# The relation bias in threshold form: each hinge as a scaled relu(d - t) or max(d, t)

## The chip, the core and the metric

The kernel runs on one NeuronCore of a Trainium2 chip. A core has five engines, each with its own queue of instructions, which wait for one another by semaphores: TensorE (PE, matrix products into PSUM), VectorE (DVE), ScalarE (ACT), GpSimd (POOL) and SyncE (SP, which here only issues DMAs). The metric is the device time of one execution in microseconds.

## The reference

A block in two stages over 16 batches of 128 rows with 128 features. The first stage runs four layers of cross attention (16 heads of 64) with a feed-forward part; the second one a self attention with a mixture of experts. The change touches one term of the first stage, the bias that is added to the scores of every head:

```python
def _attention(x, src, dist, bias, Wq, Wk, Wv, Wo, Wth, bth, Wto, bto):
    ...
    hbias = jax.nn.relu(dist[..., None] @ Wth + bth)      # 32 hinges a layer
    qs_bias = (hbias @ Wto + bto)[..., 0]
    logits = jnp.einsum('btnh,bfnh->bnft', k, q)
    logits = logits + bias + qs_bias[:, None]
    w = jax.nn.softmax(logits, axis=-1)
```

For each pair of rows with distance d the bias is the sum over k of 32 hinges w_k relu(a_k d + b_k), plus one constant and the mask. The values a, b, w differ by layer; `dist` and `mask` are the same in all four layers.

## The kernel before

All data is fp32. The first stage walks 64 units (layer by batch) in 16 groups of 4 batches. A step (g, i) works on unit i of group g, together with the projections of the unit after it and the output and feed-forward parts of the two units before it; each engine has its own list of what it does in a step, written out by hand. `walk` unrolls group 0 and the last group, and loops over the 14 between, so each engine takes a branch back at the end of a group. I call i = 0 the first step of a group, i = 1 and 2 the middle ones, i = 3 the last one.

While group g is in work, the bias of group g + 1 (4 batches, so tiles of 128 partitions by 512) is made in small parts placed among the other work:

- 24 hinges (`VEC_K`) go by way of ScalarE and VectorE. `relu` (L780) makes `relu_z = Relu(scale * dist_g + bias)` with scale and bias each a column of `cst`, into 6 slots. `term` (L938) on VectorE adds `weight * relu_z` to `bias_acc`: the first as a tensor_scalar with two column operands (L948), the other 23 as scalar_tensor_tensor, called fused below (L951). `Z_PLAN` and `TERM_PLAN` say how many of them stand at each of five places of a step; a group's first two terms stand at the second place of its first step.
- 8 hinges (`POOL_K`) go to GpSimd, two in each step: `product` (L1404, times a w, plus b w), `clamp` (L1412, min and max with bounds that are 0 or huge by the sign of w), `add` (L1419, into `pool_acc`, which begins from the mask).
- `finish_bias` (L982), the last that VectorE does in a last step, adds `bias_acc` and `pool_acc` into `bias`.

For group 0, which has no attention beside it, ScalarE and VectorE take 26 hinges and GpSimd 6.

GpSimd's other work stands in the same queue: four `norm` per step (L1393), which scale the exponentials of a quad of heads by VectorE's `inverse` (rinv, L1006), and the roots of the layer norms. VectorE's `score_quad` (L990) adds the bias to a quad's scores and finds the maximum; ScalarE's `exps` (L796) waits for it, and `inverse` waits for `exps`.

SyncE copies a layer's columns into `cst` per group: distances and a, b first (`load_dist`), GpSimd's columns next, then, when the bias of the group before is done, w and the mask (`load_wto`). At the start it loads the constants, the distances and x, waits for the constants, copies their columns, loads mask and context, and goes on to the weights.

Of the kernel before, what the change touches and what calls it, by code (L numbers as in the profile page):

```python
# [18 lines left out]
ALU = mybir.AluOpType  # L19
ACT = mybir.ActivationFunctionType  # L20
AX_X = mybir.AxisListType.X
# [23 lines left out]
START_VEC_K = 26  # L45
START_POOL_SKIP = START_VEC_K - VEC_K
POOL_FIRST = 2
Z_SLOTS = 6
# [18 lines left out]
Z_BEFORE = START_VEC_K - 1 - START_Z[-1][-1]  # L67
TERMS_BEFORE = START_VEC_K - 1 - START_TERMS[-1][-1]
# [3 lines left out]
def vec_count(g, k):  # L72

    return k if isinstance(g, int) and g == 0 else g * VEC_K + (START_VEC_K - VEC_K + k)

def pool_count(g, k):

    return k - START_POOL_SKIP if isinstance(g, int) and g == 0 else g * POOL_K + (k - START_POOL_SKIP)

def z_slot(g, k):
    return (k if isinstance(g, int) and g == 0 else START_VEC_K + k) % Z_SLOTS

C_WTH, C_BTH, C_WTO = 0, BIAS_K, 2 * BIAS_K
C_BTO = 3 * BIAS_K
C_PW, C_PB, C_HI, C_LO = [C_BTO + 1 + n * BIAS_K for n in range(4)]
C_ALL = C_BTO + 1 + 4 * BIAS_K  # L90
# [32 lines left out]
def block_program(nc, x, ctx_in, dist, mask, g_xattn, g_ffn, Wq, Wk, Wv, Wo, Wth, bth, Wto, bto,  # L123
                  Wf1, bf1, Wf2, bf2, W_qkv, b_qkv, W_gate, b_gate, W_experts, b_experts, out):
    with ExitStack() as stack:
# [32 lines left out]
        clamp_in = sb("clamp_in", [P, 2, GROUP * P])  # L158
        clamped = sb("clamped", [P, 2, GROUP * P])
        pool_acc = sb("pool_acc", [P, GROUP, P])  # L160
# [79 lines left out]
        cst_in, cst_mul, cst_ready, dist_in, cv_in, cp_in = [sem(n) for n in ("cst_in", "cst_mul", "cst_ready", "dist_in", "cv_in", "cp_in")]  # L240
        z_done, term_done, bias_done = sem("z_done"), sem("term_done"), sem("bias_done")
        pool_mul, pool_clamp, pool_sum = sem("pool_mul"), sem("pool_clamp"), sem("pool_sum")
# [60 lines left out]

        def layer_of(g, i):

            return (g + i // GROUP) >> 2
# [3 lines left out]
        def _(sp):  # L310
# [12 lines left out]
            def load_dist(g):  # L323

                load_dist_rows(g)
                load_cst(g, C_WTH, C_WTO, dist_in)

            def load_wto(g):

                load_cst(g, C_WTO, C_PW, cv_in)  # L330
                load_mask(g)
# [45 lines left out]
            for w, col in ((Wth.rearrange("l o k -> o l k"), C_WTH), (bth.rearrange("(o l) k -> o l k", o=1), C_BTH),  # L377
                           (Wto.rearrange("l k o -> o l k"), C_WTO)):
# [36 lines left out]
            wait_first(sp, consts, z_done, START_VEC_K)  # L415
# [1127 lines left out]
```

## Time and profile before

| what | value |
|---|---|
| time, median of 3 runs | 1392.51 us (1392.48 to 1393.23) |
| span of the profiled execution, first to last instruction | 1391.1 us |
| median less span, what lies around it | 1.4 us |
| TensorE busy | 1246.5 us, 90% |
| VectorE busy | 1221.8 us, 88% |
| ScalarE busy | 1062.8 us, 76% |
| GpSimd busy | 833.3 us, 60% |
| granted TensorE clock, mean | 0.968 |

A busy share is an average over stages with different limits, and a matmul's end is modelled, so a high share alone names no bound. The chain that ended last is shared out as 23% TensorE, 23% "issue", 23% VectorE, 18% ScalarE and 2% GpSimd: no engine holds it alone. The table and the chain are for the whole run; what one group and one step look like is in the rows below.

### The profile page before, as it was taken

Reading aid. Unit: us, or ns where it says so; the run is one execution under the profiler, and the core shown is the slowest. Engines: PE = TensorE matmul, PEld = TensorE weight load, DVE = VectorE, ACT = ScalarE, POOL = GpSimd, SP = SyncE. Lnnn points to the kernel's source line nnn. Section 1 sums busy time; section 2 is a strip of 40 time slices with the busy share of each in tenths; the row PEclk is TensorE's granted clock in tenths of the full one; section 3 lists DMA queues with packets and bytes.
Section 4 is the critical chain, followed back from the end, with each engine's and each line's share of the span. In section 5 each row is a group of like instructions: output and inputs, shape, how many; then the busy total and the mean of one; then the engine's idle time right before and its main releaser. Section 6 shows DMA issues by size and latency. Waiting matters only on the chain.

```text
span 1391.1 us, 39815 instructions
## 1 busy us (share of the span) xinstructions
PE 1246.5 (90%) x11184; PEld 1035.3 (74%) x11184; DVE 1221.8 (88%) x4922; ACT 1062.8 (76%) x3353; POOL 833.3 (60%) x889
## 2 busy tenths in 40 slices
PE   1599989898989899998989898989898999799998
PEld 1377878787878787787778787878777877677776
DVE  4899989898989899998989898989898988579886
ACT  4588868787878788787878787868687866478886
POOL 3677767676767677776767676767676753111110
PEclk9799999999999999999999999999999999999999
DMA  5201000102110100021100000111101000000000
GB/s 152 67 7 31 15 27 12 29 12 76 44 31 12 31 12 22 20 67 39 35 16 16 25 13 29 57 48 27 31 12 42 12 12 9 5 23 19 23 14 9
DMA packets 69115, 41.04 MB, mean 30 GB/s; under 512 B 14840, under 2 KB 63872, under 8 KB 68992
## 3 DMA queue, kind: packets, MB, share of 16 engines
q1 hardware_dynamic: 68992, 39.84, 9.9%
q14 instruction: 99, 0.81, 0.2%
q8 instruction: 24, 0.39, 0.1%
HBM read 23.29 MB, written 1.05 MB: 17 GB/s over the span
## 4 chain that ended last, share of the span: by engine, by line
PE 23%; issue 23%; DVE 23%; ACT 18%; POOL 2%; DVEq 1%; DMA 1%; ACTq 0%; SPq 0%; POOLq 0%
ACT prob L802 10%; DVE bias_acc L951 4%; PE L L688 4%; ACT relu_z L785 4%; PE O L552 3%; PE M L582 3%; DVE score L998 3%; DVE qT L1123 3%; DVE hid L1073 3%; PE M L762 2%; DVE st L1016 2%; PE M L628 2%; PE T L695 2%; PE M L560 2%; ACT probT L809 1%
## 5 line engine op out<-in xcount | busy, mean ns | idle before, releaser
L802 ACT ACTIVATE prob<-score,nmax 128x128 f32<-128x128 f32 x1024 | 396.6, 390 | 182.4 <-DVE nmax L998 182.2
L1396 POOL TENSOR_TENSOR prob<-prob,rinv 128x512 f32<-128x512 f32 x256 | 293.5, 1146 | 232.1 <-DVE rinv L1006 229.7
L951 DVE SCALAR_TENSOR_TENSOR bias_acc<-relu_z,cst,bias_acc 128x512 f32<-128x512 f32 x370 | 339.1, 917 | 9.7 <-ACT relu_z L785 0.2
L785 ACT ACTIVATE relu_z<-dist_g,cst 128x512 f32<-128x512 f32 x386 | 295.0, 804 | 17.2 <-DMA cst<-cst_all 16.9
L998 DVE CUSTOM_DVE_ANT_0 score<-L,bias 128x128 f32<-128x128 f32 x1024 | 233.6, 281 | 4.0 <-PE L L528 1.5
L802 ACT ACTIVATION_READ_ACCUMULATOR prob<-score,nmax 128x1 f32 x1024 | 193.3, 189 | 0.0
L1391 POOL TENSOR_TENSOR sd<-mv,half 128x1 f32<-128x1 f32 x128 | 105.5, 824 | 120.3 <-DVE mv L1018 117.6
L538 PE MATMUL T<-ident,prob 128*128 128x128 f32 x1024 | 164.4, 285 | 4.9 <-POOL prob L1396 4.0
L552 PEld LDWEIGHTS O<-probT,v 128*64 128x64 f32 x2048 | 109.3, 136 | 60.0 <-issue 52.4
L582 PE MATMUL M<-wv,ctxT 128*128 128x512 f32 x256 | 144.1, 645 | 7.8 <-DVE hid L1073 5.1
L528 PE MATMUL L<-kT,qT 64*128 64x128 f32 x2048 | 148.7, 285 | 0.0
L667 PEld LDWEIGHTS M<-wo,oT 128*128 128x128 f32 x1024 | 124.1, 192 | 30.6 <-issue 29.8
L560 PE MATMUL M<-hT,wq 128*128 128x128 f32 x1024 | 127.8, 279 | 20.5 <-DVE v L1106 20.5
L1428 POOL TENSOR_TENSOR pool_acc<-pool_acc,clamped 128x512 f32<-128x512 f32 x110 | 141.5, 1286 | 5.4
L560 PE MATMUL M<-ctxT,wk 128*128 128x128 f32 x1024 | 141.2, 283 | 3.8 <-issue 2.6
L552 PE MATMUL O<-probT,v 128*64 128x128 f32 x2048 | 140.1, 279 | 4.2 <-issue 2.9
L528 PEld LDWEIGHTS L<-kT,qT 64*128 64x128 f32 x2048 | 124.3, 187 | 21.2 <-issue 20.9
L560 PEld LDWEIGHTS M<-hT,wq 128*128 128x128 f32 x1024 | 120.9, 194 | 24.9 <-issue 24.9
L538 PEld LDWEIGHTS T<-ident,prob 128*128 128x128 f32 x1024 | 121.4, 146 | 22.0 <-POOL prob L1396 11.1
L628 PE MATMUL M<-h2T,wf 128*128 128x128 f32 x512 | 84.4, 315 | 58.8 <-DVE h2T L1059 58.8
L560 PEld LDWEIGHTS M<-ctxT,wk 128*128 128x128 f32 x1024 | 131.2, 200 | 4.8 <-issue 2.9
L1409 POOL TENSOR_SCALAR clamp_in<-dist_g,cst 128x512 f32<-128x512 f32 x126 | 120.1, 953 | 21.2 <-DMA cst<-cst_all 21.2
(134 smaller groups left out, 2282.8 us busy)
## 6 DMA issues: line engine op xcount, KB each, us to landing
dist_g<-in_fside_BxSxS SPq DMA_DIRECT2D x16, 256.0 KB, 2.8
mask_g<-in_mask_Bx1x1xS_ff SPq DMA_DIRECT2D x16, 256.0 KB, 3.3
ctxT<-ctxT_all SPq DMA_DIRECT2D x64, 64.0 KB, 1.9
xs<-x_all SPq DMA_DIRECT2D x64, 64.0 KB, 1.8
x_all<-xs SPq DMA_DIRECT2D x64, 64.0 KB, 1.8
wk<-in_L_xattn_Wk SPq DMA_DIRECT2D x4, 512.0 KB, 3.6
wv<-in_L_xattn_Wv SPq DMA_DIRECT2D x4, 512.0 KB, 4.7
wq<-in_L_xattn_Wq SPq DMA_DIRECT2D x4, 512.0 KB, 5.1
```

What stands on the lines that cost most here:

```text
L528: last = mm(L[r][:, m * P:(m + 1) * P], qT[64 * r:64 * r + 64, s, j, :], kT[64 * r:64 * r + 64, s, j, :], start=True, stop=True)
L538: last = nc.tensor.transpose(T[c % 2][:, m * P:(m + 1) * P], prob[:, c, m, :], ident[:, :])
L552: last = mm(O[64 * r:64 * r + 64, m * P:(m + 1) * P], v[:, i % 2, n * HD:(n + 1) * HD], probT[:, 2 * octet + r, m * P:(m + 1) * P], start= ...
L560: last = mm(dst[:, m * P:(m + 1) * P], w[:, j * P:(j + 1) * P], src, start=True, stop=True)
L582: mm((M0 if a else M1)[:, :], ctxT[:, i % 2, :], wv[:, a * 512:(a + 1) * 512], start=True, stop=True).then_inc(v_done, 1)
L667: last = mm(M2[:, 0:P], oT[:, (i - 1) % 2, j, :], wo[:, j, :], start=j == 0, stop=j == PAIRS - 1)
L785: nc.scalar.activation(relu_z[:, z_slot(g, k), :], dist_g[:, :, :], ACT.Relu, bias=cst[:, C_BTH + k:C_BTH + k + 1], scale=cst[:, C_WTH + k ...
L802: last = nc.scalar.activation(prob[:, c, m, :], score[:, c, m, :], ACT.Exp, bias=nmax[:, c, m:m + 1], scale=-1.0, accum_out=rsum[:, c, m:m ...
L951: vec.scalar_tensor_tensor(out=bias_acc[:, :], in0=relu_z[:, z_slot(g, k), :], scalar=weight, in1=bias_acc[:, :], op0=ALU.mult, op1=ALU.ad ...
L998: last = vec.tensor_tensor_reduce(out=score[:, c, m, :], in0=L[c % 2][:, m * P:(m + 1) * P], in1=bias[:, i % GROUP, :], scale=-1.0, scalar ...
L1396: gp.tensor_tensor(prob[:, c, :, :], prob[:, c, :, :], rinv[:, c, :].rearrange("p (m o) -> p m o", o=1).broadcast_to([P, 4, P]), ALU.mult) ...
L1428: gp.tensor_tensor(pool_acc[:, :, :], so_far[:, :, :], clamped[:, k % 2, :].rearrange("p (b t) -> p b t", b=GROUP), ALU.add).then_inc(pool ...
```

## The change

With t = -b / a a hinge with a > 0 is w a relu(d - t), and one with a < 0 is w |a| (relu(d - t) - (d - t)). So every hinge becomes c relu(d - t) with c = |a| w, and the parts linear in d of the falling ones are gathered in one slope `AL` and one constant `BE` per layer. On GpSimd relu(d - t) is written as max(d, t) - t, with the -t also gathered in `BE`. Hinges with a nearly 0 go whole into the constant.

- VectorE makes the new columns once, for all four layers, before the first term: 22 small instructions on up to 128 x 128, with 13 waits among them, in place of 4.
- ScalarE's relu has the constant 1.0 as its scale, and a column as its bias as before.
- VectorE's sum starts with `begin`: `AL * dist_g + mask_g` as a fused instruction; then 24 fused terms. The last sum becomes a fused one that adds `BE`.
- GpSimd makes each hinge by one tensor_scalar (max with t, times c); the first goes straight into `pool_acc`, the 7 others are added. `product` is gone, and `clamp`s stand earlier in a step.
- Group 0 is split 24 to 8 as the others are, and reads its columns straight from `cst_all`, so that SyncE copies none for it and doesn't wait for the constants.

```diff
-            wait_first(sp, consts, cst_in, 64)
-            load_cst(0, C_WTH, C_WTO, dist_in)
-            load_wto(0)
+            load_mask(0)
             sp.dma_start(c_raw[:, :, :], ctx_in.rearrange("b t d -> t b d")).then_inc(c_in, 16)
-            wait_first(sp, consts, cst_ready, 4)
-            load_cst(0, C_PW, C_ALL, cp_in)
             load_k(0)
...
-                wait(act, term_done, vec_count(g, k + 1 - Z_SLOTS))
-                nc.scalar.activation(relu_z[:, z_slot(g, k), :], dist_g[:, :, :], ACT.Relu, bias=cst[:, C_BTH + k:C_BTH + k + 1],
-                                     scale=cst[:, C_WTH + k:C_WTH + k + 1]).then_inc(z_done, 1)
+                    if isinstance(g, int) and g == 0:
+                        act.wait_ge(cst_ready, 1)
+                wait(act, term_done, term_count(g, k + 1 - Z_SLOTS) if k >= Z_SLOTS else term_count(g, k - Z_SLOTS))
+                nc.scalar.activation(relu_z[:, k % Z_SLOTS, :], dist_g[:, :, :], ACT.Relu,
+                                     bias=hinges(g)[:, C_NT + k:C_NT + k + 1], scale=1.0).then_inc(z_done, 1)
...
+            dve.wait_ge(cst_step, 6)
+            vec.reciprocal(inverse_, whole).then_inc(cst_step, 1)
+            dve.wait_ge(cst_step, 8)
+            vec.tensor_tensor(cols(C_NT), edge, inverse_, ALU.mult).then_inc(cst_ready, 1)
...
+            def begin(g):
+                dve.wait_ge(cv_in, g * 32 + 16)
+                dve.wait_ge(dist_in, g * 32 + 16)
+                if isinstance(g, int) and g == 0:
+                    dve.wait_ge(cst_ready, 4)
+                wait(dve, bias_done, g)
+                vec.scalar_tensor_tensor(out=bias_acc[:, :], in0=dist_g[:, :, :].rearrange("p b t -> p (b t)"),
+                                         scalar=hinges(g)[:, C_AL:C_AL + 1],
+                                         in1=mask_g[:, :, :].rearrange("p b t -> p (b t)"), op0=ALU.mult,
+                                         op1=ALU.add).then_inc(term_done, 1)
...
-                if k == 0:
-                    vec.tensor_scalar(bias_acc[:, :], relu_z[:, z_slot(g, k), :], weight, cst[:, C_BTO:C_BTO + 1], ALU.mult,
-                                      ALU.add).then_inc(term_done, 1)
+                vec.scalar_tensor_tensor(out=bias_acc[:, :], in0=relu_z[:, k % Z_SLOTS, :], scalar=hinges(g)[:, C_C + k:C_C + k + 1],
+                                         in1=bias_acc[:, :], op0=ALU.mult, op1=ALU.add).then_inc(term_done, 1)
...
                     for k in TERM_PLAN[i][q] if i < GROUP else ():
+                        if k == 0:
+                            begin(g + 1)
                         term(g + 1, k)
...
-                vec.tensor_tensor(bias[:, :, :], bias_acc[:, :].rearrange("p (b t) -> p b t", b=GROUP),
-                                  pool_acc[:, :, :], ALU.add).then_inc(bias_done, 1)
+                vec.scalar_tensor_tensor(out=bias[:, :, :].rearrange("p b t -> p (b t)"), in0=bias_acc[:, :],
+                                         scalar=hinges(g)[:, C_BE:C_BE + 1], in1=pool_acc[:, :], op0=ALU.add,
+                                         op1=ALU.add).then_inc(bias_done, 1)
...
             def clamp(g, k):
+                if k == 0:
+                    wait_first(pool, consts, dist_in, g * 32 + 16, bias_done, g, cp_in, g * 16)
+                    if isinstance(g, int) and g == 0:
+                        pool.wait_ge(cst_ready, 2)
+                        pool.wait_ge(cst_step, 10)
+                else:
+                    wait_first(pool, consts, pool_sum, sum_count(g, max(k - 2, 0)))
+                held = hinges(g)
+                gp.tensor_scalar(clamped[:, k % 2, :] if k else pool_acc[:, :], dist_g[:, :, :].rearrange("p b t -> p (b t)"),
+                                 held[:, C_PT + k:C_PT + k + 1], held[:, C_PT + POOL_K + k:C_PT + POOL_K + k + 1],
+                                 ALU.max, ALU.mult).then_inc(pool_clamp, 1)
...
                 if bias_too:
-                    product(g + 1, 2 * i)
                     clamp(g + 1, 2 * i)
                 if cur:
                     norm(g, i, 0)
                 if bias_too:
                     add(g + 1, 2 * i)
-                    product(g + 1, 2 * i + 1)
+                    clamp(g + 1, 2 * i + 1)
                 if cur:
                     norm(g, i, 1)
                 if bias_too:
-                    clamp(g + 1, 2 * i + 1)
                     add(g + 1, 2 * i + 1)
```

SyncE's wait before the distances of the next group gains `term_done` (that `begin` has read them), beside the relus and the clamps.

## Rows read from the trace of the kernel before

**Rows 1.** Stretch table, a middle step: us, busy us by engine (instructions), clock, DMA

```profile
664.43:680.93 16.50, 16.13 (x150) 13.59 (x150) 15.91 (x66) 14.26 (x46) 12.45 (x14) 1.00 0.04 12
```

**Rows 2.** Timeline of VectorE and TensorE, one first step: start, us, engine, line

```profile
844.65 0.18 DVE L1006 RECIPROCAL rinv<-rsum 128x4 f32<-128x4 f32 x1 [2.36 <-issue]
...
862.73 1.16 PE L628 MATMUL M<-h2T,wf 128*128 128x128 f32 x8 [0.20 <-DVE h2T L1059]
```

**Rows 3.** Timeline, the same first step: ScalarE and VectorE around quad 2

```profile
851.25 0.60 ACT L839 ACTIVATE v<-M 128x512 f32<-128x512 f32 x1 [1.16 <-PE O L552]
...
854.24 1.52 ACT L785 ACTIVATE relu_z<-dist_g,cst 128x512 f32<-128x512 f32 x2
...
854.81 0.29 DVE L998 CUSTOM_DVE_ANT_0 score<-L,bias 128x128 f32<-128x128 f32 x1
...
857.33 0.18 DVE L1006 RECIPROCAL rinv<-rsum 128x4 f32<-128x4 f32 x1 [0.39 <-ACT prob L802]
```

**Rows 4.** Timeline of ScalarE in the second stage: with and without pointer scale

```profile
1291.55 1.59 ACT L906 ACTIVATE qm<-M,bq_mask,head_mask 128x128 f32<-128x128 f32 x4
...
1292.91 1.26 ACT L872 ACTIVATE prob<-L,nmaxF 128x128 f32<-128x128 f32 x4
```

**Rows 5.** Timeline, the first step again: VectorE's first two terms, GpSimd beside them

```profile
850.66 1.32 DVE L948 TENSOR_SCALAR bias_acc<-relu_z,cst 128x512 f32<-128x512 f32 x1
...
852.11 1.05 DVE L951 SCALAR_TENSOR_TENSOR bias_acc<-relu_z,cst,bias_acc 128x512 f32<-128x512 f32 x1
...
850.40 1.29 POOL L1428 TENSOR_TENSOR pool_acc<-mask_g,clamped 128x512 f32<-128x512 f32 x1
...
851.68 0.94 POOL L1409 TENSOR_SCALAR clamp_in<-dist_g,cst 128x512 f32<-128x512 f32 x1
```

**Rows 6.** Timeline, a middle step: VectorE and GpSimd around norm 2

```profile
675.61 0.18 DVE L1006 RECIPROCAL rinv<-rsum 128x4 f32<-128x4 f32 x1
...
676.82 0.79 DVE L951 SCALAR_TENSOR_TENSOR bias_acc<-relu_z,cst,bias_acc 128x512 f32<-128x512 f32 x1
...
678.76 0.74 DVE L951 SCALAR_TENSOR_TENSOR bias_acc<-relu_z,cst,bias_acc 128x512 f32<-128x512 f32 x1
...
673.94 0.76 POOL L1416 TENSOR_SCALAR clamped<-clamp_in,cst 128x512 f32<-128x512 f32 x1
...
674.78 1.28 POOL L1428 TENSOR_TENSOR pool_acc<-pool_acc,clamped 128x512 f32<-128x512 f32 x1
...
676.02 1.04 POOL L1396 TENSOR_TENSOR prob<-prob,rinv 128x512 f32<-128x512 f32 x1
```

**Rows 7.** Timeline of VectorE from the start to the first bias

```profile
11.49 0.29 DVE L934 TENSOR_TENSOR cst_all<-cst_all 128x128 f32<-128x128 f32 x1 [11.49 <-DMA cst_all<-in_L_xattn_bto]
...
17.58 0.55 DVE L948 TENSOR_SCALAR bias_acc<-relu_z,cst 128x512 f32<-128x512 f32 x1 [5.33 <-ACT relu_z L785]
...
18.30 2.33 DVE L951 SCALAR_TENSOR_TENSOR bias_acc<-relu_z,cst,bias_acc 128x512 f32<-128x512 f32 x3 [0.17 <-ACT relu_z L785]
...
28.49 0.25 DVE L1042 RECIPROCAL ln_rs<-ln_sd 128x16 f32<-128x16 f32 x1 [0.45 <-POOL ln_sd L1518]
...
30.28 3.20 DVE L951 SCALAR_TENSOR_TENSOR bias_acc<-relu_z,cst,bias_acc 128x512 f32<-128x512 f32 x3
...
33.39 0.29 DVE L1016 BATCH_NORM_STATS2 st<-xs 128x6 f32<-128x128 f32 x1
...
57.50 0.69 DVE L987 TENSOR_TENSOR bias<-bias_acc,pool_acc 128x512 f32<-128x512 f32 x1
```

**Rows 8.** The page: DMA issues (us to landing); costliest groups (busy us, mean ns)

```profile
L951 DVE SCALAR_TENSOR_TENSOR bias_acc<-relu_z,cst,bias_acc 128x512 f32<-128x512 f32 x370 | 339.1, 917 | 9.7 <-ACT relu_z L785 0.2
...
xs<-x_all SPq DMA_DIRECT2D x64, 64.0 KB, 1.8
```

More of the change, by code:

```diff
@@ L66, with z_count, term_count, clamp_count @@
 F_FIRST_PARTS = [[0, 1], [2, 3, 4], [5, 6], [7, 8, 9], [10, 11]]
-Z_BEFORE = START_VEC_K - 1 - START_Z[-1][-1]
-TERMS_BEFORE = START_VEC_K - 1 - START_TERMS[-1][-1]
+Z_BEFORE = VEC_K - 1 - START_Z[-1][-1]
+TERMS_BEFORE = VEC_K - 1 - START_TERMS[-1][-1]
 STATS_TERMS = (4, 8)
[L72 to L87, printed above, removed]
-C_BTO = 3 * BIAS_K
-C_PW, C_PB, C_HI, C_LO = [C_BTO + 1 + n * BIAS_K for n in range(4)]
-C_ALL = C_BTO + 1 + 4 * BIAS_K
+def z_count(g, k):
+    return g * VEC_K + k
+def term_count(g, k):
+    return g * (VEC_K + 1) + 1 + k
+def clamp_count(g, k):
+    return g * POOL_K + k
+def sum_count(g, k):
+    return g * (POOL_K - 1) + k
+C_A, C_B, C_W = 0, BIAS_K, 2 * BIAS_K
+C_BTO = 3 * BIAS_K
+C_NT = C_BTO + 1
+C_C = C_NT + BIAS_K
+C_AL = C_C + BIAS_K
+C_BE = C_AL + 1
+C_PT = C_BE + 1
+C_ALL = C_PT + 2 * POOL_K
 E_HEADS = 16
@@ L302, in f_there, with hinges @@
             return not isinstance(g, int) or 0 <= GROUP * g + i < BATCHES
+        def hinges(g):
+            return cst_all[:, 0, :] if isinstance(g, int) and g == 0 else cst
         def layer_of(g, i):
@@ L931, in cols, with magnitude @@
                 return cst_all[:, :, a:a + BIAS_K]
+            slope, edge, weight = cols(C_A), cols(C_B), cols(C_W)
+            size, live, kept, whole, inverse_, falling, share, flat = [t[:, :, :] for t in prep]
+            def magnitude(out, of):
+                return vec.scalar_tensor_tensor(out=out, in0=of, scalar=-1.0, in1=of, op0=ALU.mult, op1=ALU.max)
             dve.wait_ge(cst_in, 64)
-            vec.tensor_tensor(cols(C_PW), cols(C_WTH), cols(C_WTO), ALU.mult).then_inc(cst_ready, 1)
@@ new lines, in _ @@
+            magnitude(flat, slope).then_inc(cst_step, 1)
+            dve.wait_ge(cst_step, 2)
+            vec.tensor_scalar(size, size, FLAT, TINY, ALU.mult, ALU.max).then_inc(cst_step, 1)
+            dve.wait_ge(cst_step, 3)
+            vec.tensor_tensor(live, size, flat, ALU.is_lt).then_inc(cst_step, 1)
+            dve.wait_ge(cst_step, 4)
+            vec.tensor_tensor(kept, slope, live, ALU.mult).then_inc(cst_step, 1)
+            dve.wait_ge(cst_step, 5)
+            vec.scalar_tensor_tensor(out=whole, in0=live, scalar=0.0, in1=kept, op0=ALU.is_equal, op1=ALU.add).then_inc(cst_step, 1)
@@ L1398, in norm @@
                                  ALU.mult).then_inc(normed, 1)
-            def first_k(g):
-                return START_POOL_SKIP if isinstance(g, int) and g == 0 else 0
-            def product(g, k):
-                col = VEC_K + k
-                wait_first(pool, consts, *((dist_in, (g + 1) * 32, cp_in, (g + 1) * 16) if k == first_k(g) else ()),
-                           pool_clamp, pool_count(g, k - 1))
-                gp.tensor_scalar(clamp_in[:, k % 2, :], dist_g[:, :, :], cst[:, C_PW + col:C_PW + col + 1],
-                                 cst[:, C_PB + col:C_PB + col + 1], ALU.mult, ALU.add).then_inc(pool_mul, 1)
@@ L1435, in step @@
                 if i == -1:
-                    for k in range(START_POOL_SKIP + POOL_FIRST, POOL_K):
-                        product(0, k)
+                    for k in range(POOL_FIRST, POOL_K):
                         clamp(0, k)
```

106 lines of the change are left out of this document (59 added, 47 removed).

## The prediction

> **What bounds the kernel now.** The page's busy shares come first: they call both TensorE and VectorE nearly full, so only a single step can say which wait ends last. The stretch table of a middle step of a group comes second [rows 1]: of 16.50 us TensorE works 16.13, VectorE 15.91, ScalarE 14.26 and GpSimd 12.45. VectorE's missing 0.6 us are short pauses between an instruction and the one that reads its result, so VectorE sets these steps and TensorE stands 0.37 us behind it. The timelines come third. At the start of a group's first step [rows 2] VectorE sits idle 2.36 us for "issue", at the back edge of its loop; no edit of the change is meant for that. TensorE runs on until it meets a gap of only 0.20 us, waiting for VectorE's h2T. So in the first step TensorE is 0.20 us from being the bound, and what makes VectorE late there is ScalarE [rows 3]: VectorE idles 0.39 us at 857.33 for the exponentials of quad 2, and ScalarE, released by TensorE at 851.25, worked without a pause up to them, with two relus (854.24, 1.52 us) just ahead.
>
> So I ask of every edit: does it shorten VectorE's own row of work in a middle or last step, or ScalarE's in a first step? All else is covered.
>
> **ScalarE: the relu loses its per-partition scale.** No row shows a relu with a pointer bias and a constant scale. The nearest pair [rows 4] is 128x128: four instructions with pointer bias and pointer scale take 1.59 us, four with pointer bias and constant scale 1.26, so 0.33 in three start-to-start distances and one tail: 0.08 to 0.11 each. I take 0.09; the bounds are 0 (512 elements could hide it) and 0.11. Over 24 relus and 15 prepared groups that is 32 us of ScalarE, but only the two relus before quad 2's exponentials stand on the path of a first step: 0.18 us. The scores that these exponentials also need are done at about 855.1 (854.81 + 0.29), so they could start 0.18 us sooner. VectorE then goes on that much sooner and TensorE's 0.20 us gap nearly closes; past it TensorE bounds the step. With 14 groups: -2.5 us (0 to -2.8). In middle steps the exponentials wait for VectorE's scores, and a faster ScalarE is worth nothing.
>
> **VectorE: one fused instruction more per group.** The tensor_scalar of term 0 becomes two fused ones, `begin` and term 0. A fused one alone takes 0.74 [rows 6], beside GpSimd up to 1.32 [rows 5]. That is 0.7 us more on the engine that sets most steps, 15 times, if nothing covers it. But the neighbours change. Now GpSimd's add (850.40, 1.29) and product (851.68, 0.94) run beside the pair, and the tensor_scalar ends only after the add does [rows 5]; the pair takes 2.50 us, to 853.16. After, a group's first add is gone and one clamp of about 0.77 stands there: `begin` should end at about 851.75, and two fused ones alone, 0.78 apart [rows 7], bring VectorE to about 853.4. Bounds for the three: 2.3 us (all alone) and 4.2 (each 1.32, with the pause of 0.13 that stands before 852.11). I take 2.75, near the lower end, since only one GpSimd instruction is left beside them. Up to about 0.5 us later nothing is lost, for VectorE idles 0.39 us at 857.33 and 0.1 us in two small waits before it. So: 0. If that cover is gone, each 0.1 us costs 14 x 0.1 = 1.4.
>
> **GpSimd: 15 instructions a group instead of 24.** Eight products and one add leave. Its time is worth nothing at 75% of a step; what counts is when norms start and what VectorE meets. Between norms 0 and 1 an add and a two-pointer tensor_scalar remain, as now. Between norms 1 and 2 the clamp (673.94, 0.76) goes and the add (674.78, 1.28) moves up. Norm 2 now starts only when that add ends (676.02); then it can start once VectorE's rinv (675.61, 0.18) is there, about 0.15 us sooner, and the term at 676.82 no longer meets its tail: 0.74 instead of 0.79 [rows 6]. That is 0.05 us on the engine that sets the step, in 2 steps of 14 groups: -1.4 us (0 to -1.4). In last steps VectorE is later and I count 0. What leaves before norm 0 stands beside VectorE work that reads PSUM, and counts 0 too.
>
> **The final sum** becomes a fused one: 0.69 us [rows 7] against 0.74. It is VectorE's last before the back edge, 16 times 0.05: 0.8 us, or 0 if the 2.36 us of "issue" run meanwhile; I take +0.2.
>
> **The start.** SyncE loses three copies of constants and its waits for them, so the mask, the context and the first weights are issued earlier, behind x in the same queue; VectorE's own work decides when the first step can begin. It starts when the constants have landed, at 11.49 [rows 7]. Instead of 4 small instructions it runs 22, most reading the one before: at the 0.29 of that row 6.4 us. A reciprocal of 128 elements is in no row; it lies between 0.29 and 8 times the 0.25 of one of 16, and at 1.0 makes 7.1 together. Relu 0 waits behind the ninth of them instead of a copy, which is no later. `begin` starts at 18.6, where term 0 started at 17.58. Five fused ones 0.78 apart end at 22.5, where the first four terms ended at 20.6: 1.9 us late. That carries to the normalised x: 32.2 instead of 30.28. But then one term follows where three did (3.20 us), and the first moments wait for a load of x that takes 1.8 us [rows 8]: 34.1 against 33.39. From there the same work runs to the first bias at 57.50. So +0.7 us. 
>
> **New waits.** GpSimd's clamp 0 waits for the previous bias, with norm 0 queued behind it; norm 0 needs scores of that bias, so it waits longer anyway. SyncE's next load of distances waits for `begin`, long past by then. `begin` waits for the mask where term 0 did. All 0.
>
> **Sum.** -2.5 - 1.4 + 0 + 0.2 + 0.7 = -3.0 on the span of 1391.1: 1388.1. The median of the runs is 1.4 above that span: 1389.5 us.
>
> **Rivals.** *Nothing measurable.* TensorE is 0.20 to 0.37 us behind VectorE everywhere, and the start is my softest term: with 2.5 us more there, or with the 0.18 or the 0.05 absent, the sum is between 0 and -2: 1390.5 to 1392.5. Against it: the wait of 0.39 us for ScalarE.
>
> *Less contention frees VectorE.* The 370 fused ones average 917 ns [rows 8] against 740 alone: 65 us lost beside GpSimd. If that fell with GpSimd's bias instructions, 9 of 24, it would be 24 us: 1368, or some 1380 where TensorE's 0.20 to 0.37 us a step caps it. Against it: by the timelines what goes does not stand beside fused ones in middle and last steps. It is also what the Trainium skill would have one expect (GPSIMD Engine Reference, Key points): GpSimd shares its SBUF interfaces with VectorE and contends with instructions that have two SBUF inputs. The stretched rows agree; whether it pays depends on which neighbours go.
>
> *ScalarE was the bound.* Then 32 us would go: 1360. Its 2.2 us without work in a middle step speak against it.
>
> *Slower: VectorE's extra instruction isn't covered.* If `begin` and term 0 both come out at 1.32, the three take 3.5 instead of 2.50; 0.5 of that is past the cover, 14 x 0.5 = +7, the relus' gain is lost behind it, and with -1.4 + 0.2 + 0.7 it is 1399. For it speak the 917 ns; against it the one short clamp beside three instructions. It decides from 3.2 us on for the three.
>
> **Chances.** Forecast 0.45 (its own range 1387.5 to 1391), nothing measurable 0.32, contention 0.08, ScalarE 0.02, slower 0.13. A change of 0.2%, 2.8 us, is about what can be told from none: the line is 1389.7. Of the forecast some 0.32 lies below it and 0.13 above. Faster 0.32 + 0.08 + 0.02 = 0.42; same 0.13 + 0.32 = 0.45; slower 0.13. The range leaves out most of the contention case, ScalarE's and the far half of the slower one: 1385 to 1396.
>
> **What would show it.** In the profile after: relus about 0.09 us shorter; in first steps the wait before quad 2's rinv down from 0.39 to about 0.2 and TensorE's gap before its reader of h2T near 0; middle steps 16.45 instead of 16.50; `begin` near 1.05 us; first moments near 34 us. I am wrong if `begin` and the two terms take over 3.2 us, if middle steps lengthen, if the pause at the back edge changes, or if the first bias comes more than 3 us later than now.

## The result and the profile after

| | before | after |
|---|---|---|
| time, median of 4 runs each | 1392.49 us (1386.82 to 1393.23) | 1410.78 us (1407.41 to 1414.15) |
| ratio after / before | | 1.0152, 95% interval 1.0121 to 1.0183 |
| profiled execution, span | 1391.1 us | 1408.2 us |
| busy TensorE, VectorE | 1246.5, 1221.8 us | 1256.1, 1233.5 us |
| busy ScalarE, GpSimd | 1062.8, 833.3 us | 1029.6, 875.9 us |

The change is slower by 18 us, outside the range of 1385 to 1396. Three groups of the changed kernel, by form (busy us, mean ns of one, idle time before and what ended it):

```profile
L1008 DVE SCALAR_TENSOR_TENSOR bias_acc<-relu_z,cst,bias_acc 128x512 f32<-128x512 f32 x360 | 317.0, 881 | 13.4
L799 ACT ACTIVATE relu_z<-dist_g,cst 128x512 f32<-128x512 f32 x360 | 243.0, 712 | 5.1 <-DMA cst<-cst_all 5.1
L1471 POOL TENSOR_SCALAR clamped<-dist_g,cst 128x512 f32<-128x512 f32 x105 | 237.2, 2259 | 0.0
```

Two things stand out. The relu fell by 0.09 us, as forecast, from 804 to 712 ns. But GpSimd's new clamp, which I priced at 0.77 us, takes 2.26. The fused terms even got shorter (917 in [rows 8], now 881), so longer terms don't explain the loss.

Where the time is can be read from the steps. I measure them from one copy of hT on VectorE to the next: four a group. The first two, taken together below, hold a group's end, the back edge and the first step; the other two are the middle steps. The stretch table of two groups (us, busy us by engine, granted clock of TensorE):

```profile
546.10:586.29 40.19, 35.30 (x301) 29.58 (x300) 34.08 (x133) 26.89 (x91) 26.28 (x21) 0.92 0.09 25
619.69:658.67 38.98, 34.11 (x301) 28.86 (x300) 33.94 (x133) 26.88 (x91) 26.29 (x21) 0.96 0.14 41
586.29:603.08 16.79, 16.13 (x151) 13.60 (x150) 16.09 (x67) 13.77 (x47) 13.28 (x11) 1.00 0.04 12
603.08:619.69 16.61, 16.28 (x151) 13.62 (x150) 16.00 (x66) 14.38 (x48) 13.38 (x11) 1.00 0.32 107
```

A middle step was 16.50 us [rows 1]. Now it is 16.79 and 16.61, and TensorE's work in the first has not grown: 16.13 us, as before. The pairs are 38.98 in one group and 40.19 in the other, 38.9 before on average, and they differ in the clock: the granted 0.92 and 0.96 stand for (1 - 0.92) x 2 x 40.19 = 6.4 and 3.1 us at 1.2 instead of 2.4 GHz. The clock record of the profile, which is finer, has 6.8 us in five of 13 groups and 3.4 in the others; before it was one of 13.

VectorE's timeline in a middle step shows what got longer:

```profile
667.70 0.18 DVE L1079 BATCH_NORM_AGGREGATE mv<-st 128x2 f32<-128x6 f32 x1
667.89 0.75 DVE L1008 SCALAR_TENSOR_TENSOR bias_acc<-relu_z,cst,bias_acc 128x512 f32<-128x512 f32 x1
...
670.95 0.18 DVE L1067 RECIPROCAL rinv<-rsum 128x4 f32<-128x4 f32 x1
671.14 0.75 DVE L1008 SCALAR_TENSOR_TENSOR bias_acc<-relu_z,cst,bias_acc 128x512 f32<-128x512 f32 x1
...
672.39 0.48 DVE L1092 TENSOR_SCALAR h<-xs,mv,rs 128x128 f32<-128x128 f32 x1
672.98 0.29 DVE L1059 CUSTOM_DVE_ANT_0 score<-L,bias 128x128 f32<-128x128 f32 x1
```

No instruction here is longer than before, but they start later: the two terms 0.19 us after the start of the short instruction ahead of them (0.12 before), and a score 0.11 us after the end of h, where it used to start 0.08 us ahead of that end. The kernel before, at the same h and score:

```profile
664.80 0.49 DVE L1031 TENSOR_SCALAR h<-xs,mv,rs 128x128 f32<-128x128 f32 x1
665.21 0.28 DVE L998 CUSTOM_DVE_ANT_0 score<-L,bias 128x128 f32<-128x128 f32 x1
```

No line of another engine ends these pauses. What fills the first two is not in these views, which leave out register operations and waits. The trace has them (and nothing new ahead of the score, whose pause stays open):

```
start us  us     VectorE's queue, from mv to the term behind it
kernel before
660.198   0.182  mv
660.233   0.040  register operation, carries the wait on the term before
660.318   0.787  term
changed kernel
667.696   0.182  mv
667.722   0.040  register operation
667.809   0.040  register operation, carries the wait on the term before
667.894   0.752  term
```

Here each register operation puts the next instruction 0.085 us further back. Over the whole run VectorE has 1210 of them, 874 before: 336 more, which is 24 terms x 14 looped groups.

They come from the counts in the waits. Before, terms and relus were both counted 24 a group, so the number that one term waits for on the relus is the number that the next waits for on the terms, and one register served both. `begin` now signals `term_done` as well: terms run at 25 a group, relus at 24, and in the loop, where the group is a register, each term needs a second value.

The first step and the start of the changed kernel:

```profile
855.07 0.18 DVE L1067 RECIPROCAL rinv<-rsum 128x4 f32<-128x4 f32 x1 [2.33 <-issue]
...
860.84 0.90 DVE L1000 SCALAR_TENSOR_TENSOR bias_acc<-dist_g,cst,mask_g 128x512 f32<-128x512 f32 x1
861.87 1.63 DVE L1008 SCALAR_TENSOR_TENSOR bias_acc<-relu_z,cst,bias_acc 128x512 f32<-128x512 f32 x2
...
867.74 0.18 DVE L1067 RECIPROCAL rinv<-rsum 128x4 f32<-128x4 f32 x1 [0.21 <-ACT prob L816]
...
873.48 1.16 PE L640 MATMUL M<-h2T,wf 128*128 128x128 f32 x8 [0.35 <-DVE h2T L1120]
```

```profile
17.89 0.75 DVE L1000 SCALAR_TENSOR_TENSOR bias_acc<-dist_g,cst_all,mask_g 128x512 f32<-128x512 f32 x1
...
33.16 0.29 DVE L1077 BATCH_NORM_STATS2 st<-xs 128x6 f32<-128x128 f32 x1 [1.26 <-DMA xs<-x_all]
...
53.21 4.98 DVE L1008 SCALAR_TENSOR_TENSOR bias_acc<-relu_z,cst_all,bias_acc 128x512 f32<-128x512 f32 x4
58.29 0.75 DVE L1047 SCALAR_TENSOR_TENSOR bias<-bias_acc,cst_all,pool_acc 128x512 f32<-128x512 f32 x1
```

The kernel before, its last four terms ahead of the first bias:

```profile
54.29 3.11 DVE L951 SCALAR_TENSOR_TENSOR bias_acc<-relu_z,cst,bias_acc 128x512 f32<-128x512 f32 x4
```

`begin` and two terms take 2.66 us (forecast 2.75), the wait for quad 2's exponentials is 0.21 instead of 0.39 [rows 3], and the pause at the back edge is what it was [rows 2]. But TensorE's gap before its reader of h2T is 0.35, not near 0: VectorE lost what ScalarE had gained. The first bias comes 0.8 us later, though the first moments come 0.23 us sooner than before (33.16 against 33.39 [rows 7]).

### The profile page after: what moved, and what is told of

The parts are those of the page before. It is cut to its first block, busy times and chain, and to the rows that moved or that the text cites. A ratio compares the mean times of both kernels' runs of the same rounds, so it can differ in the third digit from the quotient of the medians.

```text
span 1408.2 us, 39902 instructions
## 1 busy us (share of the span) xinstructions
PE 1256.1 (89%) x11184; PEld 1044.1 (74%) x11184; DVE 1233.5 (88%) x4954; ACT 1029.6 (73%) x3351; POOL 875.9 (62%) x751
## 3 DMA queue, kind: packets, MB, share of 16 engines
q1 hardware_dynamic: 68560, 38.62, 9.6%
## 4 chain that ended last, share of the span: by engine, by line
DVE 29%; issue 25%; PE 25%; ACT 14%; POOL 3%; DVEq 2%; DMA 2%; ACTq 0%; SPq 0%; POOLq 0%
ACT prob L816 9%; DVE bias_acc L1008 5%; DVE score L1059 5%; PE L L700 4%; PE M L640 3%; PE M L572 3%; DVE qT L1184 3%; PE M L594 2%; DVE st L1077 2%; PE O L564 2%; PE M L774 2%; DVE hid L1134 2%; PE T L707 2%; DVE probT L1098 2%; ACT relu_z L799 2%
## 5 line engine op out<-in xcount | busy, mean ns | idle before, releaser
L1457 POOL TENSOR_TENSOR prob<-prob,rinv 128x512 f32<-128x512 f32 x256 | 279.1, 1090 | 220.2 <-DVE rinv L1067 220.2
L1008 DVE SCALAR_TENSOR_TENSOR bias_acc<-relu_z,cst,bias_acc 128x512 f32<-128x512 f32 x360 | 317.0, 881 | 13.4
L799 ACT ACTIVATE relu_z<-dist_g,cst 128x512 f32<-128x512 f32 x360 | 243.0, 712 | 5.1 <-DMA cst<-cst_all 5.1
L1471 POOL TENSOR_SCALAR clamped<-dist_g,cst 128x512 f32<-128x512 f32 x105 | 237.2, 2259 | 0.0
L1452 POOL TENSOR_TENSOR sd<-mv,half 128x1 f32<-128x1 f32 x128 | 111.5, 871 | 119.3 <-DVE mv L1079 113.7
L572 PE MATMUL M<-ctxT,wk 128*128 128x128 f32 x1024 | 146.7, 290 | 4.1 <-issue 2.7
L1481 POOL TENSOR_TENSOR pool_acc<-pool_acc,clamped 128x512 f32<-128x512 f32 x112 | 149.4, 1334 | 0.6
L572 PEld LDWEIGHTS M<-ctxT,wk 128*128 128x128 f32 x1024 | 136.3, 207 | 5.2 <-issue 3.0
```

The costliest lines, as they stand in the source:

```text
L572: last = mm(dst[:, m * P:(m + 1) * P], w[:, j * P:(j + 1) * P], src, start=True, stop=True)
L799: nc.scalar.activation(relu_z[:, k % Z_SLOTS, :], dist_g[:, :, :], ACT.Relu, bias=hinges(g)[:, C_NT + k:C_NT + k + 1], scale=1.0).then_inc ...
L1008: vec.scalar_tensor_tensor(out=bias_acc[:, :], in0=relu_z[:, k % Z_SLOTS, :], scalar=hinges(g)[:, C_C + k:C_C + k + 1], in1=bias_acc[:, :] ...
L1457: gp.tensor_tensor(prob[:, c, :, :], prob[:, c, :, :], rinv[:, c, :].rearrange("p (m o) -> p m o", o=1).broadcast_to([P, 4, P]), ALU.mult) ...
L1471: gp.tensor_scalar(clamped[:, k % 2, :] if k else pool_acc[:, :], dist_g[:, :, :].rearrange("p b t -> p (b t)"), held[:, C_PT + k:C_PT + k ...
L1481: gp.tensor_tensor(pool_acc[:, :], pool_acc[:, :], clamped[:, k % 2, :], ALU.add).then_inc(pool_sum, 1)
```

## The experiments

My theory at first was the slow clamp: it makes norm 1 start late, and VectorE meets it more often. The rivals: `begin` itself, the second register of each term, the start. Times below are ratios to the kernel before, run on the same chip, with 95% intervals.

**GpSimd's pairs of operations, by themselves**, e1. A small kernel of its own, no part of the reference:

```diff
+            for rep in range(2):
+                for (a, b), r in zip(PAIRS, res):
+                    gp.tensor_scalar(r[:, :], d[:, :], c[:, 0:1], c[:, 1:2] if b else None, op(a), *([op(b)] if b else [])).then_inc(made, 1)
+                    n += 1
+                    pool.wait_ge(made, n)
...
```

> This kernel computes nothing of the reference: with nothing beside it GpSimd runs a 128x512 tensor_scalar with thirteen pairs of operations, each twice and each waiting for the one before. If the pair (max, mult) is slow by itself, it takes about 2.07 us here as well, and (mult, add) and (min, max) about 0.76. If it is slow in the changed kernel only because VectorE runs beside it, all three take 0.76 here.

Five of its groups (mean ns behind the comma; r_max_None has one operation only):

```profile
L61 POOL TENSOR_SCALAR r_max_mult<-d,c 128x512 f32<-128x512 f32 x2 | 4.1, 2067 | 0.2
...
L61 POOL TENSOR_SCALAR r_max_None<-d,c 128x512 f32<-128x512 f32 x2 | 3.1, 1564 | 0.2
...
L61 POOL TENSOR_SCALAR r_mult_mult<-d,c 128x512 f32<-128x512 f32 x2 | 1.5, 770 | 0.2
L61 POOL TENSOR_SCALAR r_mult_add<-d,c 128x512 f32<-128x512 f32 x2 | 1.5, 768 | 3.9 <-DMA c<-in_L_xattn_Wth 3.8
...
L61 POOL TENSOR_SCALAR r_min_max<-d,c 128x512 f32<-128x512 f32 x2 | 1.5, 762 | 0.2
```

The pair is slow by itself. Four pairs take 0.76 to 0.77 us: (mult, add), (add, mult), (mult, mult), (min, max). Seven take 2.07 to 2.08: (max, mult), (mult, max), (max, add), (add, max), (max, min), (min, mult), (subtract, max). One operation alone takes 1.56. So two of the old instructions, 1.53, cost less than the new one. VectorE did (max, mult) twice in the same kernel, at 0.55 each.

**The changed kernel with a quick pair**, e2.

```diff
-                                 ALU.max, ALU.mult).then_inc(pool_clamp, 1)
+                                 ALU.mult, ALU.add).then_inc(pool_clamp, 1)
```

> The changed kernel with (mult, add) in the place of (max, mult) in GpSimd's clamp, so that its eight hinges of each layer come out as d times one column plus another; all else as it is. If the slow pair is the cause, the clamp falls from 2.26 us to 0.95 or less, norm 1 of a middle step starts within 0.25 us of its rinv again, and the time is 1387 to 1394 us. If VectorE's additional fused instruction or the new start is the cause, it stays at 1405 us or more.

1411.16 us, ratio 1.0148 (1.0119 to 1.0176). The clamp fell to 0.96 us, GpSimd's busy time by 149 us, and nothing happened: middle steps 16.79 and 16.61 again. My first theory is gone.

**The kernel before with the slow pair**, e3.

```diff
-                gp.tensor_scalar(clamped[:, k % 2, :], clamp_in[:, k % 2, :], cst[:, C_HI + col:C_HI + col + 1],
-                                 cst[:, C_LO + col:C_LO + col + 1], ALU.min, ALU.max).then_inc(pool_clamp, 1)
+                gp.tensor_scalar(clamped[:, k % 2, :], clamp_in[:, k % 2, :], cst[:, C_PB + col:C_PB + col + 1],
+                                 cst[:, C_PW + col:C_PW + col + 1], ALU.max, ALU.mult).then_inc(pool_clamp, 1)
```

> The kernel before with (max, mult) in the place of (min, max) in its clamp, on the columns of the product, so that its eight hinges of each layer are other numbers; all else as it is. If the slow pair costs by itself, its clamp goes from 0.82 us to 2.1 or more, and the time is 1402 us or more, since two clamps stand in each step as in the changed kernel. If the other edits of the change make the loss, it stays at 1391 to 1395.

1450.73 us, ratio 1.0433 (1.0403 to 1.0462), middle steps 17.77. So the slow pair can cost much more than the change lost, in an order in which 24 of GpSimd's bias instructions a group stand among the norms; in the changed kernel there are 15, and e2 shows that it costs nothing there. What is late here I did not follow.

**The kernel before with relus that have the constant scale**, e4, the first term of the sum alone.

```diff
-                                     scale=cst[:, C_WTH + k:C_WTH + k + 1]).then_inc(z_done, 1)
+                                     scale=1.0).then_inc(z_done, 1)
```

> The kernel before with 1.0 as the scale of its relus (bias still a column), so that its 24 hinges of ScalarE are relu(d + b); all else as it is. By the prediction's first term the relus get 0.09 us shorter, the wait before quad 2's rinv in first steps goes from 0.39 to about 0.2 us, and the time falls by 2.5 us, to about 1390. If TensorE bounds the first steps anyway, or something else is late next, it stays within 1 us of the kernel before.

1390.70 us, ratio 0.9994 (0.9978 to 1.0010): relus of 711 ns, but -2.5 us and nothing are both inside the interval, so the time doesn't decide. The profile shows the mechanism: the wait before quad 2's rinv falls to 0.21, and TensorE's gap before its reader of h2T from 0.19 to 0.01 (mean of 13 first steps).

```profile
855.97 0.18 DVE L1006 RECIPROCAL rinv<-rsum 128x4 f32<-128x4 f32 x1 [0.21 <-ACT prob L802]
```

**`begin` on a semaphore of its own**, e5: terms are counted 24 a group again. The waits of SyncE and ScalarE on these counts (not shown) are rewritten to match.

```diff
-    return g * (VEC_K + 1) + 1 + k
+    return g * VEC_K + k
...
-                                         op1=ALU.add).then_inc(term_done, 1)
+                                         op1=ALU.add).then_inc(begun, 1)
...
-                dve.wait_ge(term_done, term_count(g, k))
+                if k == 0:
+                    dve.wait_ge(begun, g + 1)
+                else:
+                    dve.wait_ge(term_done, term_count(g, k))
```

> The changed kernel, but begin signals a semaphore of its own, so that the counts of terms and of relus are both 24 a group, as in the kernel before; the same instructions on every engine otherwise. Theory: the 24th-against-25th count made VectorE's queue work out a second register for the waits of each term (336 register operations more in the trace). Then they are gone, middle steps are back at 16.5 us and the time is 1388 to 1396 us. If begin itself, 0.99 us on VectorE, is the cause, the time stays at 1405 or more.

1388.85 us, ratio 0.9978 (0.9963 to 0.9992): all of the loss is gone, and this version beats both kernels, the one before by 0.2%. VectorE's queue has 336 register operations fewer (308 single ones and 28 fused with others); the other engines have as many of these and of waits as in the changed kernel. Its stretches, pair and middle steps of one group:

```profile
610.59:649.14 38.55, 34.11 (x301) 28.81 (x300) 33.92 (x133) 26.90 (x91) 26.56 (x21) 0.96 0.14 41
649.14:665.63 16.49, 16.14 (x151) 13.60 (x150) 15.92 (x67) 13.77 (x47) 13.18 (x11) 1.00 0.17 44
665.63:682.10 16.47, 16.08 (x151) 13.59 (x150) 15.89 (x66) 14.38 (x48) 13.26 (x11) 1.00 0.04 12
```

Its timeline at the two terms, each 0.12 us behind the start of the short one, and h with the score 0.08 us ahead of its end:

```profile
658.17 0.18 DVE L1082 BATCH_NORM_AGGREGATE mv<-st 128x2 f32<-128x6 f32 x1
658.29 0.75 DVE L1011 SCALAR_TENSOR_TENSOR bias_acc<-relu_z,cst,bias_acc 128x512 f32<-128x512 f32 x1
...
661.36 0.18 DVE L1070 RECIPROCAL rinv<-rsum 128x4 f32<-128x4 f32 x1
661.48 0.77 DVE L1011 SCALAR_TENSOR_TENSOR bias_acc<-relu_z,cst,bias_acc 128x512 f32<-128x512 f32 x1
...
662.74 0.49 DVE L1095 TENSOR_SCALAR h<-xs,mv,rs 128x128 f32<-128x128 f32 x1
663.15 0.28 DVE L1062 CUSTOM_DVE_ANT_0 score<-L,bias 128x128 f32<-128x128 f32 x1
```

**The kernel before with two counts**, e6: the reverse, alone.

```diff
+def term_count(g, k):
+    more = 1 if k >= 1 else 0
+    return k + more if isinstance(g, int) and g == 0 else g * (VEC_K + 1) + (START_VEC_K - VEC_K + k + more)
...
-                    dve.wait_ge(term_done, vec_count(g, k))
+                    dve.wait_ge(term_done, term_count(g, k))
...
-                                      ALU.add).then_inc(term_done, 1)
+                                      ALU.add).then_inc(term_done, 2)
```

> The kernel before with the count of its terms raised by 2 at a group's first term, so that it runs at 25 a group beside 24 for the relus; nothing else is changed, and no engine's arithmetic. By the theory of the second register it loses what the change lost: 336 register operations more, middle steps of 16.6 to 16.8 us, 1402 to 1410 us. If begin or GpSimd's clamp is the cause, it stays at 1391 to 1395.

1406.33 us, ratio 1.0104 (1.0080 to 1.0128). An edit of a count alone costs 14 us: 308 register operations more on VectorE (22 terms of 14 groups here) and not one on another engine, middle steps of 16.61.

**e5 with the quick pair**, e7, whose edit is that of e2, and **e5 without `begin`**, e8, which also leaves out SyncE's wait for it.

```diff
-                        if k == 0:
-                            begin(g + 1)
                         term(g + 1, k)
...
+                if k == 0:
+                    vec.tensor_scalar(bias_acc[:, :], relu_z[:, k % Z_SLOTS, :], weight, hinges(g)[:, C_AL:C_AL + 1], ALU.mult,
+                                      ALU.add).then_inc(term_done, 1)
```

> As the run with begin on its own semaphore, and with (mult, add) in the place of (max, mult) in GpSimd's clamp, so that its eight hinges of each layer come out as d times one column plus another. It prices the slow pair once VectorE's queue is no longer what is late: if GpSimd was only hidden behind the queue, this is 3 us or more below that run; if not, within 2 us of it.

> As the run with begin on its own semaphore, but without begin: the first term is a tensor_scalar again, which adds the column AL, and the mask and the part linear in d are left out of the bias. It prices VectorE's one more instruction a group: if begin is covered, as forecast, within 2 us of that run; if it costs its 0.7 us in each of 15 groups, about 10 us below.

e7: 1388.52 us, ratio 0.9979 (0.9964 to 0.9993), no more than e5. The slow pair costs nothing in the new order. e8: 1399.38, ratio 1.0047 (1.0030 to 1.0064), slower by 10 where I expected equal or faster. Middle steps stay at 16.48; the pairs are 39.5 instead of 38.6. Its first step has pauses that e5 has not:

```profile
641.05 0.18 DVE L1063 RECIPROCAL rinv<-rsum 128x4 f32<-128x4 f32 x1 [0.85 <-ACT prob L814]
...
649.32 0.18 DVE L1075 BATCH_NORM_AGGREGATE mv<-st 128x2 f32<-128x6 f32 x1 [0.47 <-DVE st L1073]
```

The first is only VectorE that arrives sooner; the second, 0.47 us where 0.10 is usual, is another pause that no other engine explains. Behind it TensorE's gap before its reader of h2T is 0.39 us in each of 13 first steps, 5 us in all, where e5 has 0.01; three longer stretches at 1.2 GHz are some 4 us more. So taking `begin` out gains nothing, but what makes the pause stays open, and e8 gives `begin` no price.

**Relus counted 25 a group too**, e9.

```diff
-    return g * VEC_K + k
+    return g * (VEC_K + 1) + k
...
-                                     bias=hinges(g)[:, C_NT + k:C_NT + k + 1], scale=1.0).then_inc(z_done, 1)
+                                     bias=hinges(g)[:, C_NT + k:C_NT + k + 1], scale=1.0).then_inc(z_done, 2 if k == VEC_K - 1 else 1)
```

> The changed kernel with begin still counted among the terms, but the last relu of a group counted twice, so that relus and terms both run at 25 a group: the same edit of order and arithmetic as the change, and one register value for both waits of a term. By the theory of the second register it is as fast as the kernel with begin on its own semaphore, 1386 to 1392 us, with some 900 register operations on VectorE. If moving begin's signal was what helped there (SyncE waits for it too), it stays at 1405 us or more.

1409.97 us, ratio 1.0136 (1.0111 to 1.0161): a miss, and the most useful run. The register operations did go, to 888. But a term now waits for one fresh number twice, and in the trace the operation that works the number out carries neither wait; one of them became an instruction of its own: 336 more of these, 2131 against 1795.

```
start us  us     VectorE's queue with relus and terms at 25
665.733   0.182  mv
665.759   0.040  register operation
665.847   0.021  wait on one of the two
665.912   0.751  term
```

So it isn't register arithmetic alone that costs: a wait in its place, a second instruction in VectorE's queue ahead of each term, does as well. By the expectation, 1405 or more would mean that moving `begin`'s signal was the help in e5, since SyncE waits for it too. e6 speaks against that: it has no `begin` and leaves SyncE's waits alone, and loses 14 us. The Trainium skill (Perfetto Trace Analysis, Identifying Dependency Chains) says that an instruction which waits on several engines may have a wait instruction put ahead of it; these rows show one, and its price of 0.065 us.

**Terms in pairs**, e10: an even term waits for two relus, and 168 of the register operations go.

```diff
...
+                elif k % 2:
+                    dve.wait_ge(term_done, term_count(g, k + 1))
+                else:
+                    dve.wait_ge(term_odd, term_count(g, k))
+                if k % 2 == 0:
+                    dve.wait_ge(z_done, z_count(g, k + 2))
...
```

> The kernel with begin on its own semaphore, and the terms in pairs: an even one waits for two relus at once, and even and odd terms count on two semaphores by 2, so that one register serves two terms. 168 register operations fewer again on VectorE, the same arithmetic. If each of them costs, the time falls by 3 us or more; if only those cost that VectorE's queue has no time for, and the kernel with its own semaphore has none such left, it stays within 1.5 us of it. A wait for two relus instead of one may also cost.

1489.79 us, ratio 1.0697 (1.0668 to 1.0726). The wait for the second relu stops VectorE:

```profile
707.39 1.22 DVE L1014 SCALAR_TENSOR_TENSOR bias_acc<-relu_z,cst,bias_acc 128x512 f32<-128x512 f32 x1 [0.82 <-ACT relu_z L799]
```

The edit also made 336 waits of their own, 2131 against 1795. Whether fewer operations than in e5 would help is not answered by it.

**e5 with a column of ones as the relus' scale**, e11.

```diff
-                                     bias=hinges(g)[:, C_NT + k:C_NT + k + 1], scale=1.0).then_inc(z_done, 1)
+                                     bias=hinges(g)[:, C_NT + k:C_NT + k + 1], scale=ones[:, 0:1]).then_inc(z_done, 1)
```

> The kernel with begin on its own semaphore, and a column of ones as the scale of the relus in place of the constant: the relus' 0.09 us come back, the same values. By the prediction's first term it is 2.5 us slower than that kernel, about 1391; if the gain came from elsewhere (VectorE's neighbours on GpSimd, the start), within 1 us of it.

1392.60 us, ratio 1.0001 (0.9984 to 1.0017) against e5's 0.9978 (0.9963 to 0.9992): 0.0023, or 3.2 us slower; 2.5 were expected. The two intervals overlap at their ends, so the size is rough. TensorE's gap before its reader of h2T is back at 0.20, and the wait before quad 2's rinv at 0.40:

```profile
642.79 0.18 DVE L1073 RECIPROCAL rinv<-rsum 128x4 f32<-128x4 f32 x1 [0.40 <-ACT prob L819]
```

**One wait more ahead of some terms of e5**: in the middle steps, e12, and in first and last steps, e13, with (0, 3) for (1, 2).

```diff
+                        if k and i in (1, 2):
+                            dve.wait_ge(begun, g + 2)
                         term(g + 1, k)
```

> The kernel with begin on its own semaphore, and one wait more (on begin, long satisfied) ahead of each of the 12 terms of a group's two middle steps: 12 short instructions more in VectorE's queue, no arithmetic. If each costs only where it stands, the middle steps grow from 16.48 to 16.6 to 16.8 us, the first steps stay, and the time is 1392 to 1396 us. If a group that gets 0.4 us longer also meets longer stretches of TensorE at its lower clock (6.8 instead of 3.4 us) in its first steps, some of them there grow by 1.2 us and the time is 1400 or more.

> The kernel with begin on its own semaphore, and the same wait ahead of the 11 terms after the first of a group's first and last step. If each costs only where it stands, the middle steps stay at 16.48 us and the pair around VectorE's back edge grows by about 0.35 us: 1392 to 1396 us. If it is the lower clock that answers to a longer group, 1400 or more here too; if waits in these steps are covered by TensorE, within 1.5 us of the kernel with begin on its own semaphore.

e12: 1396.2 us, ratio 1.0045 (1.0022 to 1.0067), its runs from 1388.8 to 1402.8. e13: 1399.31, ratio 1.0055 (1.0036 to 1.0075), between the two times that were expected for it. The profiled execution of e12 is its shortest:

```profile
610.59:649.08 38.49, 34.01 (x301) 28.71 (x300) 33.83 (x134) 26.88 (x91) 26.58 (x21) 0.96 0.15 41
649.08:665.70 16.62, 16.13 (x151) 13.60 (x150) 15.96 (x67) 13.73 (x47) 13.30 (x11) 1.00 0.18 44
665.70:682.26 16.56, 16.09 (x151) 13.59 (x150) 15.90 (x66) 14.36 (x48) 13.33 (x11) 1.00 0.04 12
```

Here the wait costs where it stands and only there: middle steps +0.13 and +0.09, the pair as in e5, no long stretch of the lower clock. In e13 the middle steps stay (16.47, 16.52) and the pairs grow to 39.1, two of 13 with 6.8 us of it. That e12's other runs are up to 14 us longer was not seen in a profile; the three longest have a mean granted clock of 0.961 to 0.964, the profiled one 0.970.

The profiles side by side (register operations and waits of VectorE; middle steps and the mean pair of the looped groups in us; groups of 13 with 6.8 us at 1.2 GHz; TensorE's mean gap before its reader of h2T in the first steps, us). e2 is like the changed kernel. The times are medians on several chips, on which the kernel before takes 1391.5 to 1393.1:

| kernel | reg. ops | waits | middle | pair | long | gap | time, us |
|---|---|---|---|---|---|---|---|
| before | 874 | 1794 | 16.50, 16.50 | 38.9 | 1 | 0.19 | 1392.5 |
| after | 1210 | 1795 | 16.79, 16.61 | 39.5 | 5 | 0.34 | 1410.8 |
| e4 before, constant scale | 874 | 1794 | 16.50, 16.50 | 38.8 | 1 | 0.01 | 1390.7 |
| e5 own semaphore | 902 | 1795 | 16.48, 16.48 | 38.6 | 0 | 0.01 | 1388.9 |
| e6 before, two counts | 1182 | 1809 | 16.61, 16.61 | 39.4 | 4 | 0.34 | 1406.3 |
| e7 own semaphore, quick pair | 902 | 1795 | 16.48, 16.48 | 38.6 | 1 | 0.08 | 1388.5 |
| e8 without begin | 874 | 1795 | 16.48, 16.48 | 39.5 | 3 | 0.39 | 1399.4 |
| e9 25 and 25 | 888 | 2131 | 16.76, 16.58 | 39.4 | 4 | 0.29 | 1410.0 |
| e10 terms in pairs | 734 | 2131 | 18.32, 18.32 | 41.9 | 13 | 0.88 | 1489.8 |
| e11 ones as scale | 902 | 1795 | 16.48, 16.48 | 38.9 | 1 | 0.20 | 1392.6 |
| e12 waits, middle | 902 | 1963 | 16.62, 16.57 | 38.5 | 0 | 0.08 | 1396.2 |
| e13 waits, ends | 902 | 1949 | 16.47, 16.52 | 39.1 | 2 | 0.27 | 1399.3 |

The groups of e7 price the clock within one execution: two of its pairs have no time at 1.2 GHz and take 37.8 us, ten have 3.4 us of it and take 38.5 to 38.8, one has 6.8 and takes 39.8.

## Why the prediction was wrong, step by step

**The step that failed is "New waits ... All 0".** It asked of each new wait what stands behind it and found nothing late, but it looked at when a wait ends, not at what it takes to issue, and the waits of the 24 terms, whose count `begin` changes, are not in its list. `begin`'s signal on `term_done` put a second instruction ahead of 24 terms a group, 0.07 us each behind a short one. With the count put right the kernel takes 1388.85 us, and I had forecast 1389.5; with the count alone spoiled, the kernel before loses 14 of the 18 us. Of the signs of being wrong one came, and it is this one: middle steps got longer, from 16.50 to 16.79 and 16.61 us.

**How 0.07 us a term became 20 us.** By the profiles, the looped part is 17.6 us longer in the changed kernel than in e5, the span 21.2. Of the 17.6, the middle steps, which VectorE sets, make (0.31 + 0.13) x 13 = 5.7. Some 0.19 x 13 = 2.5 of it is the pause before the score, which only the changed kernel, e2 and e9 have; e6 and e12, without it, price the second instruction at 0.09 to 0.13 a middle step. The pairs make (39.48 - 38.62) x 13 = 11.2: five with the longer stretch at 1.2 GHz are some 1.2 us above the other eight, 6 us, and apart from that all 13 are 0.4 above e5's, 5 us. Of the 0.4, 0.33 is TensorE's gap before its reader of h2T (0.34 against 0.01). Some 4 us more stand in the second stage, whose code is the same; its granted clock is 0.95 in the changed kernel and 0.97 in e5. That the second instruction makes middle steps and TensorE's gap longer is shown, by e5, e6, e9, e12 and e13 from both sides. That it makes the clock stay low for longer is not: e8 has three such groups without it, and the one profile of e12 none with it. What decides whether a group gets 3.4 or 6.8 us at 1.2 GHz stays open.

**The forecast's number, which e5 meets, is partly luck.** Against the kernel before, e5's pairs without a long stretch are 38.62 instead of 38.79 us, 2 us over 13, which is the relus' term; but a long stretch that only the kernel before has is 1.2 us, and its second stage, where no edit stands, is 1.5 us longer.

**ScalarE's term (-2.5)** was right in its mechanism: relus of 0.71 us, the wait from 0.39 to 0.21, TensorE's gap from 0.19 to 0.01 (e4), back at 0.20 in e11, where the scale costs 3.2 us, roughly.

**`begin` (0)** was right in its place, 2.66 us for the three against 2.75, and TensorE's gap of 0.01 in e5 leaves it nothing to cost in a first step; e8 could not price it.

**GpSimd (-1.4)** was wrong in price: the clamp takes 2.26 us, not 0.77, since I took the row of another pair of operations for it. It cost nothing (e2, e7); GpSimd's load in a middle step rose only from 12.45 to 13.28 and 13.38 us. Middle steps gained 0.02 us in e5, not 0.05; that the gain stands at norm 2 was not followed.

**The start (+0.7)** came out by luck: the first bias is 0.8 us later in the changed kernel and 0.7 in e5, but not by the path forecast. VectorE's 22 instructions took 6.4 us instead of 7.1 (the reciprocal 0.95, near the 1.0 that was taken and under the estimate of 1.07), so `begin` stands at 17.89 instead of 18.6 and the first moments at 33.16, not 34.1. "From there the same work" failed: the last four terms before the first bias take 4.98 us, beside GpSimd's clamps and adds, where they took 3.11.

**The final sum (+0.2)** takes 0.75 us (0.69 in [rows 7]), and the pause behind it is 2.33 us instead of 2.36 [rows 2]: whether its 0.06 cost anything is not told apart.

**The slower rival** had the right side and the wrong mechanism: not `begin` beside GpSimd, but the count that it signals.

## What to carry to other kernels

Count the short instructions ahead of an engine's work as you count its work: in a loop whose counts live in registers, two semaphores that are counted at the same rate share a value, and one more signal on one of them takes that away. An edit that only signals, on an engine that sets the steps, is not free. Price an operation by a row of that very operation; where no row has it, measure it alone before building on it.

## What the runs showed of the hardware that was not expected

- On GpSimd a 128x512 tensor_scalar takes 0.77 us with some pairs of operations and 2.07 with others, and a single operation takes 1.56, longer than a quick pair. The Trainium skill (GPSIMD Engine Reference, Engine selection), which compares GpSimd with VectorE, calls work with one input roughly line rate; VectorE took 0.55 us for (max, mult) of this size in e1, which four of the eleven pairs come near and seven do not.
- On VectorE a register operation sets the next start back by 0.085 us and a wait that stands alone by 0.065, where the instruction ahead is as short as 0.18. Behind one of 0.34 us (h) the changed kernel's term starts as early as before.
- Scores of the changed kernel, of e2 and of e9 show 6.2 us of "issue" idle time in all, 0.9 in the kernel before, e5, e6, e12 and e13: some 0.39 us more in the last step of each looped group. The pause before the score of a middle step, too short for that count, comes with it. These three have 439 VectorE instructions in the loop, the others 413 to 438. What makes these pauses, and the 0.47 us one of e8, stays open.
